# Mamba and attention layer on one core: GpSimd multiplies a fifth unit of each batch by C

## The reference

```
# block 1 (mamba)
shift, scale, gate = split(silu(c) @ ada_w.T + ada_b, 3)
xn = layernorm(x) * (1 + scale) + shift
x_in, z = split(xn @ in_proj_w.T, 2)                    # 512 channels each
u  = silu(causal_conv(x_in, 4 taps) + conv_b)
dt_r, B, C = split(u @ x_proj_w.T, [64, 16, 16])
dt = softplus(dt_r @ dt_proj_w.T + dt_proj_b)
h[t] = h[t-1] * exp(dt[t] * A) + dt[t] * u[t] * B[t]    # 16 states per channel
y[t] = sum over the 16 states of h[t] * C[t]
x1 = x + gate * (((y + u * D) * silu(z)) @ out_proj_w.T)
# block 2 (linear attention, 8 heads)
q, k, v = ln(x1) @ Wq + bq, ... ; q = softmax(q) in heads, k = softmax(k) over time, v masked
y = q @ (k.T @ v);  h = silu(ln(y) * (1 + scale2) + shift2)
out = x1 + h @ W_out + b_out
```

## Time and profile before

| | us |
|---|---|
| median of 3 runs | 571.92 (571.04 to 574.27) |
| the profiled execution | 571.14 |
| its span, first to last instruction | 569.1 |
| busy in it: VectorE, GpSimd, TensorE, ScalarE | 517.4, 453.1, 431.1, 405.3 |
| first scan starts, last product by C ends | 34.5, 536.0 |

### The profile page before, as it was taken

How to read it: one execution, slowest core, us unless ns; L and a number is a source line. 1 busy time by engine, 2 the same in 40 slices (tenths; PEclk the granted TensorE clock), 3 DMA queues, 4 the chain that set the end, 5 groups by cost and what they waited for, 6 DMA issues and landing times. The chain is left out here.

```text
span 569.1 us, 7357 instructions
## 1 busy us (share of the span) xinstructions
PE 431.1 (76%) x2444; PEld 353.9 (62%) x2444; DVE 517.4 (91%) x568; ACT 405.3 (71%) x887; POOL 453.1 (80%) x318
## 2 busy tenths in 40 slices
PE   8979656768787768679677668779687767755897
PEld 6657445456685656558565557668585656654775
DVE  2379999999999999999999999999999999999653
ACT  2695668588857989498966988498857987585434
POOL 4049979989997899978997899978996899993121
PEclk9978778899788999988899988899788998899999
DMA  8294044003310044003230153003220044000001
GB/s 255 77 314 140 0 150 128 22 29 118 105 77 1 28 167 150 1 28 119 96 104 1 31 178 137 0 29 139 91 88 1 10 178 139 1 0 20 0 1 37
DMA packets 22365, 45.37 MB, mean 80 GB/s; under 512 B 3684, under 2 KB 13556, under 8 KB 22328
## 3 DMA queue, kind: packets, MB, share of 16 engines
q1 hardware_dynamic: 22328, 44.92, 23.7%
HBM read 42.52 MB, written 2.39 MB: 79 GB/s over the span
## 5 line engine op out<-in xcount | busy, mean ns | idle before, releaser
L520 POOL TENSOR_TENSOR hs<-dtu,Br 128x1024 f32<-128x1024 f32 x127 | 297.1, 2363 | 9.3 <-DMA Br<-bc_rows 9.0
L681 ACT ACTIVATE ring<-dt,Aneg 128x256 f32<-128x256 f32 x512 | 213.1, 466 | 82.0 <-DVE hs L893 74.2
L886 DVE TENSOR_TENSOR_SCAN ring<-ring,hs 128x1024 f32<-128x1024 f32 x97 | 221.2, 2281 | 1.7 <-ACT ring L681 1.5
L1236 PE MATMUL sums<-ident,hs 128*128 128x128 f32 x1024 | 148.1, 300 | 57.7 <-DVE hs L893 57.7
L1236 PEld LDWEIGHTS sums<-ident,hs 128*128 128x128 f32 x1024 | 130.9, 156 | 72.7 <-DVE hs L893 70.1
L893 DVE TENSOR_TENSOR hs<-ring,Cr 128x1024 f32<-128x1024 f32 x97 | 118.7, 1224 | 3.3
L529 POOL TENSOR_TENSOR hs<-hs,Cr 128x1024 f32<-128x1024 f32 x31 | 73.2, 2362 | 42.5 <-DVE hs L886 42.5
L886 DVE TENSOR_TENSOR_SCAN hs<-ring,hs 128x1024 f32<-128x1024 f32 x31 | 70.3, 2268 | 0.0
L1304 PE MATMUL PY<-wqkvo,xT 128*128 128x256 f32 x168 | 46.3, 425 | 0.0
L1231 PE MATMUL sums<-ident,uD 128*128 128x128 f32 x64 | 15.1, 325 | 36.6 <-DVE ygT L900 36.6
L1304 PEld LDWEIGHTS PY<-wqkvo,xT 128*128 128x128 f32 x168 | 37.5, 223 | 6.7
(11 more groups left out here) (204 smaller groups left out, 674.4 us busy)
## 6 DMA issues: line engine op xcount, KB each, us to landing
Br<-bc_rows SPq DMA_DIRECT2D x32, 512.0 KB, 5.0
Cr<-bc_rows SPq DMA_DIRECT2D x32, 512.0 KB, 4.1
xg<-in_x SPq DMA_DIRECT2D x8, 256.0 KB, 2.8
out<-fin SPq DMA_DIRECT2D x7, 256.0 KB, 4.3
hs<-in_ada_wT SPq DMA_DIRECT2D x3, 512.0 KB, 5.2
win<-in_in_wT SPq DMA_DIRECT2D x2, 512.0 KB, 7.5
hs<-in_W_emb SPq DMA_DIRECT2D x2, 512.0 KB
gate<-gate_rows SPq DMA_DIRECT2D x8, 128.0 KB, 3.0
```

The lines of the kernel that those rows point to most:

```text
L520: nc.gpsimd.tensor_tensor(hs[:, g % DBUF], dtu[:, b % 2, dc, :].unsqueeze(1).to_broadcast([P, NQ, T]), Br[:, NQ * q:NQ * q + NQ, :], ALU.m ...
L681: ins = nc.scalar.activation(ring[:, g % 2, j, :], dt[:, b % 2, dc, :], ACT.Exp, scale=Aneg[:, c:c + 1])
L886: V.tensor_tensor_scan(driven if by_pool(g) else decays, decays, driven, 0.0, ALU.mult, ALU.add).then_inc(s_scan_done, 1)
L1236: ins = M(YT[:, c, :], hs[:, g % DBUF, j, P * c:P * c + P], ident[:, :], is_transpose=True, start=False, stop=(q == UPC - 1 and j == NQ - ...
```

## The change

Beside the fifth unit the diff holds edits of the start, of batch 1's slots, of TensorE's order in step 3 and of the end.

1. `by_pool` takes in unit 3, and begins with unit 5 of batch 0; so seven more units are GpSimd's, unit 3 of batches 1 to 7. Unit 3 closes its group's sums, so it is not `deferred`: TensorE sums it in its turn and waits there for GpSimd.
2. TensorE issues `out_proj` in step 3 ahead of the sums of unit 3.
3. Start: the two ada loads have a semaphore each and the matmuls of the first don't wait for the second; 32 fillers, not 40; u and the softplus of batch 0 in smaller parts; VectorE makes dt and dt*u of group 0 before the first unit and those of group 1 (`second_inputs`) behind unit 1.
4. Batch 1: `modulated`, the taps and in_proj_2 one unit later.
5. End: the last batch's v is masked by VectorE; the transposes of batch 6's k go behind the last transposes back, q times att of batch 6 behind the first half of x1 turned, the transposes for batch 6's output behind q times att of batch 7; fewer fillers.

```diff
 def by_pool(g):
-    return g % U in (1, 5, 9, 13) and g > 1
+    return g % U in (1, 3, 5, 9, 13) and g > 3
+def deferred(g):
+    return by_pool(g) and g % UPC != UPC - 1
 def summed_after(g):
-    return g - 1 if g >= 1 and by_pool(g - 1) else None
+    return g - 1 if g >= 1 and deferred(g - 1) else None
 def sums_until(g):
-    return g + 2 if by_pool(g) else g if g >= 1 and by_pool(g - 1) else g + 1
+    return g + 2 if deferred(g) else g if g >= 1 and deferred(g - 1) else g + 1
...
+            def silu_u_half(h):
+                act.wait_ge(s_tap_done, 6 * (h + 1))
+                half = slice(2 * h, 2 * h + 2)
+                nc.scalar.activation(u[:, 0, half], conv[:, half], ACT.Silu).then_inc((s_u_first, s_u_ready)[h], 1)
+            def softplus_first():
+                act.wait_ge(s_u_ready, 1)
+                nc.scalar.activation(dt[:, 0, 0], PX[:, 0, :], ACT.Relu)
+                nc.scalar.activation(vln[:, 0], PX[:, 0, :], ACT.Abs).then_inc(s_first_abs, 1)
...
+                nc.scalar.activation(dt[:, 0, 1], PX[:, 1, :], ACT.Relu).then_inc(s_vpos_ready, 1)
+                nc.scalar.activation(vln[:, 1], PX[:, 1, :], ACT.Abs).then_inc(s_vabs_ready, 1)
...
# ScalarE, last steps
-                copy_kT(LAST_B - 1)
                 last_yg((3,), z_bank(LAST_B))
+                copy_kT(LAST_B - 1)
...
-                mask_v(LAST_B)
...
# VectorE
+            def second_inputs():
+                dve.wait_ge(s_vln_ready, 1)
+                V.tensor_tensor(dt[:, 0, 1], dt[:, 0, 1], vln[:, 1], ALU.add).then_inc(s_dt_sum, 1)
+                dve.wait_ge(s_dt_sum, 1)
+                V.tensor_tensor(dtu[:, 0, 1], dt[:, 0, 1], u[:, 0, 1], ALU.mult).then_inc(s_dtu_ready, 1)
+                dve.wait_ge(s_dtu_ready, 1)
+                V.memset(dt[:, 0, 1, 0:1], BIG).then_inc(s_dt_ready, 1)
...
+                dve.wait_ge(s_v_mm, NB)
+                for c in range(TC):
+                    V.tensor_scalar(vm[:, c, :], v_bank(LAST_B)[:, c, :], pcol("mask", ...), None, ALU.mult)
...
# TensorE
-                keep_on(40, True)
+                keep_on(32, True)
                 pe.wait_ge(s_sc_ready, 1)
-                pe.wait_ge(s_ld_ada, 32)
-                setup_mods(pm, adaT, 0).then_inc(s_mod_mm, 1)
+                setup_mods(pm, adaT, 0, s_ld_ada).then_inc(s_mod_mm, 1)
...
                 last_back((3,), z, DC)
+                transpose_k(b - 1)
...
-                q_times_att(b - 1)
-                keep_on(10)
+                keep_on(3)
                 pe.wait_ge(s_xh_ready, TC * b + 1)
                 turn_half(z, xhat, 0)
-                keep_on(3)
+                q_times_att(b - 1)
+                keep_on(2)
...
-                pe.wait_ge(s_yh_ready, TC * b)
-                transposes(PZ, xh).then_inc(s_yT_mm, 1)
                 pe.wait_ge(s_att_ready, KD * NB)
...                                                       # q times att, both halves
+                pe.wait_ge(s_yh_ready, TC * b)
+                transposes(PZ, xh).then_inc(s_yT_mm, 1)
                 output(b - 1)
...
             for g in range(FIRST, NB * U):
-                if 0 <= g < NB * U and not by_pool(g):
+                b = due(g, 19)
+                if b is not None:
+                    out_proj(b)
+                if 0 <= g < NB * U and not deferred(g):
                     sum_states(g // U, g % U)
```

More of the change, by code:

```diff
@@ L198, in build @@
         s_ld_ident = sem("ld_ident")
-        s_ld_ada = sem("ld_ada")
+        s_ld_ada = [sem(f"ld_ada{i}") for i in range(2)]
         s_ld_emb = sem("ld_emb")
@@ L821, in _ @@
                                    (33, copy_kT), (38, normalize2)):
-                    late = 1 if step in (conv_last_tap_0, conv_last_tap_1) else 0
+                    late = 2 if step in (conv_last_tap_0, conv_last_tap_1) else 1 if step is modulated else 0
                     b = due_soon(g, slot) if step is normalize0 else due_by(g, slot, late)
+                    if (b, step) == (0, softplus_parts_1):
+                        continue
                     if b is not None:
                         step(b)
-                if g == 1:
+                if g == 2:
                     softplus_log(0, 1)
@@ L864, in first_inputs @@
             def first_inputs():
[L866 to L871, removed]
+                dve.wait_ge(s_first_vln, 1)
+                V.tensor_tensor(dt[:, 0, 0], dt[:, 0, 0], vln[:, 0], ALU.add).then_inc(s_first_sum, 1)
+                dve.wait_ge(s_first_sum, 1)
+                V.tensor_tensor(dtu[:, 0, 0], dt[:, 0, 0], u[:, 0, 0], ALU.mult).then_inc(s_first_dtu, 1)
+                dve.wait_ge(s_first_dtu, 1)
+                V.memset(dt[:, 0, 0, 0:1], BIG).then_inc(s_first_dt, 1)
                 dve.wait_ge(b_loaded[0], 16)
@@ L1089, in _ @@
                     scan_unit(g // U, g % U)
+                if g == 1:
+                    second_inputs()
                 for dc in range(DC):
@@ L1122, in transposes, with setup_mods @@
                 return ins
-            def setup_mods(pm, w, lo):
+            def setup_mods(pm, w, lo, loads=None):
                 for j in range(2 * KD):
+                    if loads and j % KD == 0:
+                        pe.wait_ge(loads[j // KD], 16)
                     for k in range(KC):
@@ L1201, in x_proj @@
                     pe.wait_ge(s_pool_const, 8)
+                    pe.wait_ge(s_u_first, 1)
+                else:
+                    pe.wait_ge(s_u_ready, b + 1)
                 for k in range(DC):
+                    if (b, k) == (0, DC // 2):
+                        pe.wait_ge(s_u_ready, 1)
                     ins = M(PX[0:RANK + 2 * N, 0, :], wxp[:, k, :], u[:, b % 2, k, :], start=(k == 0),
@@ L1478, in _ @@
                     last_back((2,), PX, 3)
-                for slot, step in ((17, transpose_back), (19, out_proj), (-19, transpose_x), (-18, in_proj_0), (-16, in_proj_1), (-14, in_proj_2),
+                for slot, step in ((17, transpose_back), (-19, transpose_x), (-18, in_proj_0), (-16, in_proj_1), (-14, in_proj_2),
                                    (-13, in_proj_3), (39, output), (-9, x_proj), (-8, dt_proj_0), (-6, dt_proj_1),
@@ L1483, in _ @@
                                    (35, transpose_y)):
-                    b = due_by(g, slot, -2 if step is in_proj_1 else 1 if step is in_proj_2 else 2 if step is in_proj_3 else 0)
+                    b = due_by(g, slot, -2 if step is in_proj_1 else 2 if step in (in_proj_2, in_proj_3) else 0)
                     if b is not None and not (b == LAST_B - 1 and step in (k_times_v, q_times_att)):
```

54 lines of the change are left out of this document (45 added, 9 removed).

## The result

The changed kernel took 578.91 us in the median of four runs (577.12 to 580.75), the kernel before 571.96 beside it (571.04 to 574.27). The ratio is 1.0114, with an interval of 1.0085 to 1.0144: slower by 7 us, where 573.4 had been forecast and 576.3 was the top of the range. The profiled execution is the 580.75 one (span 578.9), so its trace shows some 1.8 us more than the median; the one of the kernel before lies 0.8 us under its own.

What follows compares the result with a forecast made beforehand. VectorE, busy 91% of the span, was taken as the bound unless something else comes late. Terms 5.4 - 0.8 - 1.0 - 2.1 = +1.5 us gave 573.4 us on the median's scale, range 570.5 to 576.3.

Steps and rivals of the forecast that it cites:

- Part 2: Steady batches, TensorE's and VectorE's side: `gate_y` waits 0.2 us, hidden behind the residual; shorter waits for decays give -0.8 us.
- the rest of the batch keeps its distances: Steady batches after `stats1`: nothing else comes later; GpSimd takes up 1.4 us of its delay at unit 9.
- Part 3: The start: earlier modulation matmuls and xdbl, against the cost of `second_inputs`: -1.0 us, bounds -2.0 and +0.9.
- the later slots: Batch 1's taps and projections issued later: work moves within gapless stretches, costing nothing.
- Part 1: Steady batches, GpSimd's side: the new product delays `residual`, so `stats1` waits and VectorE's saving is lost: +5.4 us.
- rival B: Faster: GpSimd absorbs its delay before it reaches `stats1`, so VectorE's saving stays: -9.7, 562.2 us, chance 0.1.
- its two readings: `out_proj` ahead of unit 3's sums takes 3.62 us at full clock or 5.30 at half clock; same sum by both.
- rival C: Slower: `gate_y` decides, with `out_proj` and unit 3's sums at half clock: +3.3 more, 576.7 us, chance 0.1.
- the 1.94: Start, up to the first scan: modulation matmuls -1.1 us, u and x_proj in halves -0.84.
- The straight line over sizes: `second_inputs` on VectorE: two 256-element operations at 0.42 us each, estimated from 512 and 1024 elements; 0.95 with issue.
- Part 4: The end: reordered transposes of k and xh shorten the wait for the last `gate_y`: -2.1 us, bounds -2.7 and -0.5.
- Rival A: Slower: `residual` late as forecast, but half clock leaves start at 0 and end at -0.7: +3.9, 575.8 us, chance 0.18.

Runs made afterwards that it cites:

- e1: The kernel before with only unit 3's product moved to GpSimd and `out_proj` ahead of its sums, start and end untouched: 580.9 us, ratio 1.0143.
- e4: The changed kernel with `rstd2` ahead of unit 3's product in GpSimd's order instead of behind it: 570.12 us, ratio 0.9961.
- e9: The changed kernel with 24 dummy matmuls on TensorE behind the sums of unit 6 of batches 1 to 7: 576.18 us, ratio 1.0083.
- e5: The changed kernel with `rstd2` ahead of unit 3's product, `in_proj_2` of batch 1 a step earlier and GpSimd held in batch 0: 568.34 us, ratio 0.9955.
- e7: The changed kernel with `out_proj` back behind the sums of unit 3: 580.38 us, ratio 1.0142.
- e6: The changed kernel with GpSimd's input for unit 3 of batch 0 held until VectorE's `second_inputs` is done: 578.81 us, ratio 1.013.
- e3: The changed kernel with `in_proj_2` of batch 1 one step earlier on TensorE, in its old slot: 578.85 us, ratio 1.0121.
- e2: The changed kernel with four units per batch on GpSimd as before (1, 5, 9, 13), all other edits kept: 571.16 us, ratio 0.9976.
- e10: e5 with `stats1` a step later in VectorE's order, behind unit 7 instead of unit 6: 564.34 us, ratio 0.988.

## Why the prediction was wrong

The direction was right, the size was not: +1.5 us forecast, +7 measured in the medians, +9.6 between the two profiled executions. Two steps failed. Part 2 had it that "the rest of the batch keeps its distances"; the runs showed 4.7 us of waits for TensorE there. Part 3 put the start at −1.0, with the later slots at nothing and `second_inputs` at 0.95; the profile showed +2.7. Step by step, on the profiled scale:

**Part 1 held.** It said that `stats1` would start 12.30 us behind unit 3's scan and wait 1.5 to 2.1 us; it started 12.35 us behind and waited 2.06. Taken from the starts of the scans, VectorE's delay grew between unit 3 and unit 7 by 0.60, 0.71, 0.69, 1.13, 0.77, 0.70 and 1.15 us in batches 1 to 7: 5.75 where +5.4 stood. GpSimd's idle time before the new product, forecast at 2.4, was 2.5 in batches 4 to 6, 3.0 and 4.2 in 2 and 3, and 0.4 in 7. e1 and e4 show the cause from both sides. With it rival B fell: GpSimd's queue did not absorb the delay.

**Part 2 held where it looked.** `gate_y` waits 0.17 us in batches 2 to 7 (forecast 0.2) and 1.34 in batch 1; `out_proj` at 3.62 us is the first of its two readings, so rival C fell. What it called "the rest of the batch keeps its distances" did not hold: `fin` waits three times for 1.02 us, and the conv taps of batch 3 once for 1.66, behind matmuls at the low clock. That is 4.7 us, of which the prediction had none. The steps are its own: it counted TensorE's gap that `out_proj` fills, and not the one that the 2.06 us wait of `stats1` opens on TensorE a unit later. e9 closes that gap, and the output is back at 1.89. This accounts for the 3.06 us of `fin`, though not by a fixed price: the same wait of `stats1` left `fin` in time in batches 3 to 5. It does not account for the 1.66 of the taps. They come behind `in_proj` matmuls for which the granted clock was 0.51 from 232 to 239, well away from that gap; e9 has a wait of 1.71 in batch 4, and e5, where `stats1` hardly waits, has two. Why they come in one execution and not in another stays open.

**Part 3, the start, failed.** It gave −1.0 up to the first scans, with "the later slots of batch 1's taps and projections move work within gapless stretches: nothing". Measured: +2.7 by the end of batch 0, which is −0.7 at the first scan, +2.4 for `second_inputs`, +2.5 at unit 6 and −1.6 at unit 8.
- The first scan came 0.68 us sooner, not 1.94. The modulation matmuls did start sooner, at 7.95 in place of 9.15, but took 4.70 us in place of 3.71, and e7, which has the same code up to there, took 3.64 and had its first scan at 30.84: TensorE's clock in that stretch differs between executions of one and the same code, so the number of fillers is not shown to be its cause. Nor is the 1.94 refuted: the old start has its first scan at 34.48 and 36.48 (the kernel before and e1), the new one anywhere from 30.84 to 34.58 in twelve kernels, 33.3 in the mean. One pair of executions can't price this term.
- `second_inputs` cost 2.4 us, not 0.95. The straight line over sizes was right for the operation, 0.41; the 1.4 more are GpSimd's product beside it. The trace of the kernel before held a row of this kind. VectorE, then GpSimd, around unit 9 of batch 0:

```profile
71.52 1.78 DVE L1016 TENSOR_SCALAR m1s<-mods,par 128x8 f32<-128x8 f32 x1
73.22 0.22 DVE L1016 TENSOR_SCALAR m1b<-mods,par 128x8 f32<-128x8 f32 x1
...
63.97 9.31 POOL L520 TENSOR_TENSOR hs<-dtu,Br 128x1024 f32<-128x1024 f32 x4
```

  Eight columns in 1.78 us, until the last of four input products ends at 73.28, and in 0.22 right after. The Trainium skill's "SBUF — State Buffer", section "SBUF: two separate sides", has the rule: VectorE in an operation with two SBUF inputs (or in a mode that takes both ports) and GpSimd exclude each other from one pair of ports, and the later one is blocked until the other's instruction is over. The trace of e6 agrees: 0.41. The addition of `second_inputs` reads two tiles in SBUF; that `m1s` runs in such a mode no row shows. The scans and products by C read `ring` in PSUM, and none of them is slowed in any trace here: one scan takes 2.22 to 2.30 us, one product 1.22 or 1.23. At this place the changed kernel, being later, gains: its `m1s` took 0.23. That is the −1.6, and the prediction had it at nothing too.
- The slots of batch 1 did matter. `in_proj_2` one step later costs the wait before unit 6, 2.39 us here and 0.85 where TensorE was at its full clock in this stretch (e9), since in ScalarE's order the copy of z stands ahead of `decays(6)`. The prediction itself asks who stands behind a wait; it did not ask it here. e3 removes this wait. TensorE in e9:

```profile
57.43 1.88 PE L1258 MATMUL PX<-win,xnT 128*128 128x512 f32 x4
```

**Part 4 held.** From the start of the last scan to the end of the span the changed kernel is 2.2 us shorter, where −2.1 stood; the transposes of k follow without the 1.59 us of the earlier trace rows.

Summed up on the profiled scale: +2.7 start and batch 0 (−1.0 forecast), +5.75 (5.4), +4.7 `fin` and taps (0), −1.1 all other waits (−0.8), −2.2 end (−2.1): 9.85 against 9.8 between the spans. The two failed steps are 3.7 and 4.7 us. Rival A had the right direction, for another reason: the end gave what it was to give, and its 575.8 is still 3 us short. None of the rivals held the two failed steps.

What stays open: why the clock at the start differs between executions of the same code, and with it how the 1.8 us between the profiled execution and the median come about; and what makes the taps wait in some executions. The shares of the two failed steps are read from one execution, and e2 and e9 show that the one in batch 0 varies between executions by over 1.5 us.

## What to carry to other kernels

When an engine's in-order queue takes on work that has to wait for another engine, look at what is queued behind it: here four operations of 0.2 to 0.7 us ahead of the waiting product or behind it decided over 8.8 us. "A slot later within a gapless stretch" is only free if each engine that reads the result has nothing urgent behind that read. And before an operation is put on VectorE, look at its operands: with two in SBUF it lasted until GpSimd's instruction was over, and an edit that frees it in one place can move it into another. Last, a gap opened on one engine can cost a second time, at the pace of the matmuls behind it.

## What the runs showed of the hardware that had not been expected

- A VectorE operation of 256 elements with both inputs in SBUF took 0.41 us beside an idle GpSimd and 1.54 to 1.99 us beside a GpSimd product of 2.35 us, the end of which it awaited. Small operations of 8 columns took up to 3.22 us (e10) in place of 0.22, longer than any single GpSimd product there. The profile books this as the operation's duration, not as idle time before it.
- After TensorE had idled for 4.58 us, the matmuls that followed ran at the lower clock (1.97 us for eight transposes and 3.45 for the output, against 1.10 and 1.89 in e9). In three of the six batches with such a wait, 2 us on one engine thus cost another 1.02 us at a place some 10 us further on.
- The start has two courses for the same instructions. TensorE in the changed kernel, then in e7:

```profile
7.95 4.70 PE L1198 MATMUL PX<-cT,hs 128*128 128x8 f32 x32
12.51 1.01 PE L1183 MATMUL sums<-ones 97*128 97x256 bf16 x4
```

```profile
7.46 3.64 PE L1198 MATMUL PX<-cT,hs 128*128 128x8 f32 x32
10.96 0.60 PE L1183 MATMUL sums<-ones 97*128 97x256 bf16 x4
```

  In the first, four fillers take 1.01 us and the first scan starts at 33.81; in the second 0.60, and it starts at 30.84, 3.6 us sooner than in the kernel before. The granted clock from 8 to 12 and from 12 to 16 us was 0.79 and 0.50 in the first, 1.00 in both stretches in the second; in the kernel before it was 1.00 and 0.70, so the 3.6 us are not the edit's alone.
